# A graph network on one core: own messages transposed apart and joined on VectorE, one subtraction on GpSimd, shorter stage orders

## What is computed

```python
# layer 0 (twice): out[dst] = sum over edges of dinv[src]*dinv[dst]*(x @ W)[src], plus b
# layer 2:
att = sigmoid(xs @ W_att[:d] + xd @ W_att[d:] + b_att)     # xs = x[src], xd = x[dst]
messages = (xs @ W_msg + b_msg) * att
aggregated = segment_sum(messages, dst)
gi = aggregated @ W_ih.T + b_ih ;  gh = x @ W_hh.T + b_hh
r, z = sigmoid(i_r + h_r), sigmoid(i_z + h_z)
n = tanh(i_n + r * h_n)
h_new = (1 - z) * n + z * x                                # then batch norm over the nodes
# layer 3: segment_sum(x[src], dst) @ W_neigh.T + b_neigh + x @ W_self.T + b_self
```

## Time and profile before

| | |
|---|---|
| time, median of 3 runs | 5524.07 us (5515.52 to 5529.74) |
| the profiled execution: its own time, its span | 5528.89 us, 5527.1 us |
| mean granted TensorE clock in it | 0.956 |
| busy: PE, DVE, ACT, POOL | 87%, 70%, 49%, 55% |
| gcn_second, from 855 us | about 557 us |
| attend, from 3985 us | about 745 us |
| combine, from 4975 us to the end | 552 us |

### The profile page before, as it was taken

How to read it: one execution, slowest core, us unless ns; L and a number is a source line. 1 busy time by engine, 2 the same in 40 slices (tenths; PEclk the granted TensorE clock), 3 DMA queues, 4 the chain that set the end, 5 groups by cost and what they waited for, 6 DMA issues and landing times. The chain is left out here.

```text
span 5527.1 us, 107663 instructions
## 1 busy us (share of the span) xinstructions
PE 4833.4 (87%) x28685; PEld 3861.5 (70%) x28685; DVE 3842.1 (70%) x11930; ACT 2711.7 (49%) x6605; POOL 3016.8 (55%) x2962
## 2 busy tenths in 40 slices
PE   4499996666799989999999998888799999787887
PEld 4488885555688867777777775777566666676877
DVE  8567775776688855555555554788678888785766
ACT  2644444655433322222222222777677777573555
POOL 0177765777677743333433332777466665007776
PEclk9999997777899989999999998999999999998999
DMA  4889994554577754444444443788877666794554
GB/s 153 273 246 274 273 271 142 151 148 145 179 238 237 235 171 156 151 149 148 154 153 152 146 152 96 222 243 245 244 227 223 218 221 208 250 313 131 151 151 142
DMA packets 551179, 1075.25 MB, mean 195 GB/s; under 512 B 110995, under 2 KB 118202, under 8 KB 547962
## 3 DMA queue, kind: packets, MB, share of 16 engines
q1 hardware_dynamic: 451194, 854.46, 46.4%
q0 software_dynamic: 99840, 219.14, 16.1%
HBM read 712.24 MB, written 360.98 MB: 194 GB/s over the span
## 5 line engine op out<-in xcount | busy, mean ns | idle before, releaser
L841 POOL DMA_INDIRECT s_rows<-t_h,s_index x416 | 523.9, 1259 | 833.9 <-DVE s_index L834 732.9
L841 POOL DMA_INDIRECT g_rows<-t_x,g_index x416 | 426.8, 1026 | 382.3 <-issue 361.1
L841 POOL DMA_INDIRECT cb_rows<-t_x,cb_index x416 | 395.4, 950 | 432.0 <-DVE cb_index L834 309.8
L841 POOL DMA_INDIRECT at_rows<-t_m,at_index x416 | 434.5, 1044 | 301.1 <-DVE at_index L834 191.0
L841 POOL DMA_INDIRECT s_rows<-t_v,s_index x416 | 407.1, 979 | 211.5 <-issue 125.9
L841 POOL DMA_INDIRECT s_rows<-t_x,s_index x416 | 420.7, 1011 | 152.4 <-issue 118.2
L841 POOL DMA_INDIRECT g_rows<-t_h,g_index x416 | 402.3, 967 | 171.2 <-issue 124.4
L905 PE MATMUL bank<-s_onehot,s_hi 128*128 128x80 f32 (+9 forms) x1758 | 437.5, 289 | 48.8 <-DVE s_lo L876 27.3
L1724 DVE TENSOR_TENSOR s_rout<-bank,s_x 128x512 f32<-128x512 f32 x98 | 67.8, 692 | 586.9 <-PE bank L1668 586.9
L905 PE MATMUL bank<-g_onehot,g_rows 128*128 128x80 f32 (+9 forms) x1172 | 298.5, 420 | 195.0 <-DMA g_rows<-t_h,g_index 184.5
L905 PE MATMUL bank<-s_onehot,s_lo 128*128 128x80 f32 (+9 forms) x1758 | 432.0, 286 | 0.0
(11 more groups left out here) (335 smaller groups left out, 13286.1 us busy)
## 6 DMA issues: line engine op xcount, KB each, us to landing
s_scale<-inv_d SPq DMA_DIRECT2D x196, 256.0 KB
t_h<-s_hout SPq DMA_DIRECT2D x98, 512.0 KB
s_own<-t_h SPq DMA_DIRECT2D x98, 512.0 KB
t_m<-s_mout SPq DMA_DIRECT2D x98, 264.0 KB
at_own<-t_m SPq DMA_DIRECT2D x98, 264.0 KB
t_x<-so_x SPq DMA_DIRECT2D x98, 256.0 KB, 4.5
g_own<-t_x SPq DMA_DIRECT2D x98, 256.0 KB
g_scale<-dinv_d SPq DMA_DIRECT2D x98, 256.0 KB
```

The lines of the kernel that those rows point to most:

```text
L841: pool.indirect_dma_start(out=self.rows[:, self.ring(q) + k, :], out_offset=None, in_=self.table[0:NPAD, :], in_offset=bass.IndirectOffset ...
```

## The change

In `attend`: `mine` is no longer multiplied into the bank of the sums. A new TensorE piece `flip` transposes it into a bank of its own (bank 6), ACT `hold` now copies that bank to `own_t`, and a new VectorE piece `join` computes agg = own_t x own + sums in one pass out of the bank. The candidate's matmul of all tiles now goes to bank 5 (it was bank 5 or 6 in turn), so it waits for the blend of the tile just before. The subtraction x2 - n moves from VectorE's `move` to GpSimd's `part`, into a tile `diff`. r, z and n get four buffers each, and lags and list orders change. In `gcn_second` and `combine` only lags and orders change.

```diff
 # gcn_second
-                    (9, lambda q: store(sp, q, group_of(t_x1[0:NPAD, :], q.t), xout[q.u][:, :], ln.applied,
+                    (6, lambda q: store(sp, q, group_of(t_x1[0:NPAD, :], q.t), xout[q.u][:, :], ln.applied,
...
-                over_groups(pe, [(3, turn), (1, sums)])
+                over_groups(pe, [(1, sums), (2, turn)])
...
-                over_groups(act, [(2, hold), (4, weight), (6, lambda q: ln.root(act, q)), (8, apply)])
+                over_groups(act, [(2, hold), (4, lambda q: ln.root(act, q)), (3, weight), (5, apply)])
...
-                e.on_vector(dve, [(7, lambda q: ln.invert(dve, q)), (5, add), (0, lambda q: e.prepare(dve, q))])
+                e.on_vector(dve, [(0, lambda q: e.prepare(dve, q)), (4, lambda q: ln.invert(dve, q)), (3, add)])
 # attend
-                e.fetch(pool)
+                def part(q):
+                    pool.wait_ge(tanhed, q.t + 1)
+                    if not is_first(q.t):
+                        wait_for(pool, moved, q.t - 1)
+                    pool.tensor_tensor(diff[q.u][:, :], x2[q.d % XS][:, :], ng[q.r][:, :], ALU.subtract)\
+                        .then_inc(parted, 1)
+
+                over_groups(pool, [(0, lambda q: e.gather(pool, q)), (7, part)], XS)
...
-                                 (10, lambda q: store(sp, q, slab_of(hnt, q.t), hn[q.u][:, :], moved, stored))],
+                                 (11, lambda q: store(sp, q, slab_of(hnt, q.t), hn[q.u][:, :], moved, stored))],
...
                 def sums(q):
                     e.fetched(pe, q)
+                    if not is_first(q.t):
+                        pe.wait_ge(agged, q.t - 1)
+                    e.sum_by_feature(pe, q, [bank[q.u]]).then_inc(e.summed, 1)
+
+                def flip(q):
                     pe.wait_ge(mailed, q.t + 1)
-                    if not is_first(q.t):
-                        pe.wait_ge(agged, q.t - 1)
-                    e.sum_by_feature(pe, q, [bank[q.u]], close=False)
+                    if not (isinstance(q.t, int) and q.t < 1):
+                        pe.wait_ge(copied, q.t)
                     for b in range(BLK):
-                        last = pe.matmul(nodes(bank[q.u])[:, b, :], mine[q.u][:, b, :],
-                                         id_own[:, :], start=False, stop=(b == BLK - 1),
-                                         skip_group_check=True)
-                    last.then_inc(e.summed, 1)
+                        last = pe.transpose(bank[6][:, b * P:(b + 1) * P], mine[q.u][:, b, :], ident[:, :])
+                    last.then_inc(turned, 1)
...
-                    if not is_first(q.t):
-                        pe.wait_ge(mixed, q.t - 1)
-                    pe.matmul(bank[5 + q.u][:, :], wih_s[:, 2 * P:3 * P], agg[q.u][:, :], start=True, stop=True)\
+                    if not (isinstance(q.t, int) and q.t < 1):
+                        pe.wait_ge(mixed, q.t)
+                    pe.matmul(bank[5][:, :], wih_s[:, 2 * P:3 * P], agg[q.u][:, :], start=True, stop=True)\
                       .then_inc(joined, 1)
 
-                over_groups(pe, [(5, gates), (3, sums)], XS)
+                over_groups(pe, [(5, gates), (3, sums), (2, flip)], XS)
...
                 def hold(q):
-                    act.wait_ge(e.summed, q.t + 1)
-                    if not is_first(q.t):
-                        act.wait_ge(joined, q.t - 1)
-                    act.activation(planes(agg[q.u]), nodes(bank[q.u]), ACT.Copy).then_inc(agged, 1)
+                    act.wait_ge(turned, q.t + 1)
+                    if not is_first(q.t):
+                        act.wait_ge(agged, q.t - 1)
+                    act.activation(own_t[q.u][:, :], bank[6][:, :], ACT.Copy).then_inc(copied, 1)
...
-                over_groups(act, [(4, hold), (6, candidate), (1, open_), (2, weigh), (5, gate)], XS)
+                over_groups(act, [(3, hold), (6, candidate), (1, open_), (1, weigh), (5, gate)], XS)
...
+                def join(q):
+                    dve.wait_ge(copied, q.t + 1)
+                    dve.wait_ge(e.summed, q.t + 1)
+                    if not is_first(q.t):
+                        dve.wait_ge(joined, q.t - 1)
+                    dve.scalar_tensor_tensor(out=planes(agg[q.u]), in0=planes(own_t[q.u]), scalar=own[:, 0:1],
+                                             in1=nodes(bank[q.u]), op0=ALU.mult, op1=ALU.add).then_inc(agged, 1)
...
                 def move(q):
 
-                    dve.wait_ge(tanhed, q.t + 1)
+                    dve.wait_ge(parted, q.t + 1)
                     if not is_first(q.t):
                         dve.wait_ge(stored[q.u], q.n * 16)
-                    dve.tensor_tensor(hn[q.u][:, :], x2[q.d % XS][:, :], ng[q.u][:, :], ALU.subtract)\
+                    dve.tensor_tensor(hn[q.u][:, :], diff[q.u][:, :], zg[q.r][:, :], ALU.mult)\
                        .then_inc(link3, 1)
...
-                e.on_vector(dve, [(2, choose), (1, look), (6, move), (5, blend)], ahead=2)
+                e.on_vector(dve, [(4, join), (2, choose), (0, look), (7, move), (5, blend)], ahead=2)
 # combine
-                    (8, leave)])
+                    (6, leave)])
...
-                over_groups(pe, [(1, sums), (3, dense)])
+                over_groups(pe, [(1, sums), (2, dense)])
...
-                over_groups(act, [(2, hold), (5, lambda q: ln.root(act, q)), (7, apply)])
+                over_groups(act, [(2, hold), (4, lambda q: ln.root(act, q)), (5, apply)])
...
-                e.on_vector(dve, [(6, lambda q: ln.invert(dve, q)), (4, add), (0, lambda q: e.prepare(dve, q))])
+                e.on_vector(dve, [(0, lambda q: e.prepare(dve, q)), (4, lambda q: ln.invert(dve, q)), (3, add)])
```

More of the change, by code:

```diff
@@ L1897, in attend @@
             agg = ph.pair("agg", [P, GRP])
-            r, zg, mix, ng = (ph.pair(n, [P, GRP]) for n in ("r", "z", "mix", "n"))
+            own_t, diff, mix = (ph.pair(n, [P, GRP]) for n in ("own_t", "diff", "mix"))
+            r, zg, ng = (ph.pair(n, [P, GRP], n=4) for n in ("r", "z", "n"))
+            turned, copied, parted = ph.sem("turned"), ph.sem("copied"), ph.sem("parted")
             hn = ph.pair("hn", [P, GRP])
@@ L1990, in weigh @@
                     if not is_first(q.t):
-                        act.wait_ge(e.summed, q.t - 1)
+                        act.wait_ge(turned, q.t - 1)
                     for b in range(BLK):
@@ L1997, in hold @@
                 def hold(q):
-                    act.wait_ge(e.summed, q.t + 1)
+                    act.wait_ge(turned, q.t + 1)
                     if not is_first(q.t):
-                        act.wait_ge(joined, q.t - 1)
-                    act.activation(planes(agg[q.u]), nodes(bank[q.u]), ACT.Copy).then_inc(agged, 1)
+                        act.wait_ge(agged, q.t - 1)
+                    act.activation(own_t[q.u][:, :], bank[6][:, :], ACT.Copy).then_inc(copied, 1)
                 def gate(q):
                     act.wait_ge(crossed, q.t + 1)
-                    if not is_first(q.t):
-                        act.wait_ge(moved, q.t - 1)
+                    if not is_first(q.t, 4):
+                        act.wait_ge(moved, q.t - 3)
                     a, b = GATES[q.u]
-                    act.activation(r[q.u][:, :], bank[a][:, :], ACT.Sigmoid, bias=brz_c[:, 0:1])
-                    act.activation(zg[q.u][:, :], bank[b][:, :], ACT.Sigmoid, bias=brz_c[:, 1:2])\
+                    act.activation(r[q.r][:, :], bank[a][:, :], ACT.Sigmoid, bias=brz_c[:, 0:1])
+                    act.activation(zg[q.r][:, :], bank[b][:, :], ACT.Sigmoid, bias=brz_c[:, 1:2])\
                        .then_inc(opened, 1)
@@ L2013, in candidate @@
                     act.wait_ge(mixed, q.t + 1)
-                    act.activation(ng[q.u][:, :], mix[q.u][:, :], ACT.Tanh, bias=bih_c[:, 2:3])\
+                    act.activation(ng[q.r][:, :], mix[q.u][:, :], ACT.Tanh, bias=bih_c[:, 2:3])\
                        .then_inc(tanhed, 1)
-                over_groups(act, [(4, hold), (6, candidate), (1, open_), (2, weigh), (5, gate)], XS)
+                over_groups(act, [(3, hold), (6, candidate), (1, open_), (1, weigh), (5, gate)], XS)
             @block.vector
@@ L2042, in blend @@
                     dve.scalar_tensor_tensor(out=mix[q.u][:, :], in0=hx[q.d % XS][:, :], scalar=bhh_c[:, 2:3],
-                                             in1=r[q.u][:, :], op0=ALU.add, op1=ALU.mult).then_inc(link, 1)
+                                             in1=r[q.r][:, :], op0=ALU.add, op1=ALU.mult).then_inc(link, 1)
                     dve.wait_ge(link, q.t + 1)
                     dve.wait_ge(joined, q.t + 1)
-                    dve.tensor_tensor(mix[q.u][:, :], mix[q.u][:, :], bank[5 + q.u][:, :], ALU.add)\
+                    dve.tensor_tensor(mix[q.u][:, :], mix[q.u][:, :], bank[5][:, :], ALU.add)\
                        .then_inc(mixed, 1)
                 def move(q):
-                    dve.wait_ge(tanhed, q.t + 1)
+                    dve.wait_ge(parted, q.t + 1)
```

(9 more changed lines are left out.)

2 lines of the change are left out of this document (1 added, 1 removed).

## The result

| | before | after |
|---|---|---|
| median of the runs made side by side, us | 5525.59 (7 runs, 5515.52 to 5529.74) | 5542.50 (7 runs, 5537.01 to 5546.27) |
| the profiled execution, us | 5528.89 | 5546.27 |
| its span, us | 5527.1 | 5544.5 |

The ratio is 1.0029, with a 95% interval of 1.0018 to 1.0041: the kernel has become 17 us **slower**, at the edge of the 0.3% that the prediction named. The forecast was 5499 us, and faster.

What follows compares the result with a forecast made beforehand. Gathers were taken to bound gcn_second and combine, TensorE attend, and GpSimd attend after the change. The profiled 5528.9 us less 20 (attend) and 8 (ends) gave 5501, stated as 5499 us; range 5468 to 5544.

Steps and rivals of the forecast that it cites:

- Bound and waits before: Kernel before: gathers bound gcn_second and combine; TensorE bounds attend, busy all 600 us, at 7.23 us a tile.
- The four numbers close behind TensorE: Attend, us a tile: VectorE 6.35, ScalarE 5.59, GpSimd 5.8, the round over ScalarE and VectorE 6.7.
- 1, TensorE: Attend: four passes fewer save 0.45 us a tile, 44 us over 98 tiles; TensorE's tile becomes 6.78 us.
- 2, VectorE: Attend: subtraction of 0.691 us goes, join of 0.747 comes; VectorE's tile becomes 6.41 us.
- rival C: Attend: GpSimd's subtraction takes 1.16 us of VectorE every tile, giving 7.57 us a tile; slower, 5554 us; chance 0.13.
- 2, the waits on VectorE: Attend: the 42.9 us wait for the store goes; the join's wait for its tile's sums costs nothing.
- 3, ScalarE and bank 5: Attend: ScalarE's copy from bank 6 and bank 5 alone for the candidate cost nothing if the round stays under 6.78 us.
- 4, GpSimd: Attend: subtraction costs 1.46 us a tile between gathers, between 0.85 and 2.01; GpSimd sets the pace, attend ends 20 us earlier.
- 5, the ends: Ends of gcn_second and combine: fewer applies after the last root, 4 us each, 8 us together, between 0 and 12.

Runs made afterwards that it cites:

- e1: The changed kernel with only the subtraction back on VectorE, GpSimd only gathering; 5524.75 us, 0.9999 of the kernel before.
- e2: The kernel before with only the new lags and orders of gcn_second and combine, attend untouched; 5513.09 us, 0.9979 of the kernel before.
- f3: The changed kernel with the subtraction on VectorE and the own rows' load ahead of x2's; 5497.67 us, 0.9960 of the kernel before.
- f2: The changed kernel with only the subtraction back on VectorE, run in a later series; 5518.43 us, 0.9988 of the kernel before.
- f1: The changed kernel itself, run again as control in the later series; 5541.56 us, 1.0030 of the kernel before.
- f4: The changed kernel, GpSimd's subtraction included, with the own rows' load ahead of x2's; 5532.88 us, 1.0014 of the kernel before.
- e6: The kernel before with only the subtraction on GpSimd, r, z, n in four buffers, move and store a step later; 5526.02 us, 1.0000 of before.
- e5: The kernel before with new orders in gcn_second and combine, own messages as transposes adding into the bank of the sums; 5502.35 us, 0.9957.

## Why the prediction was wrong

By its own steps:

- **Bound and waits before**: right as far as they go. The four numbers close behind TensorE were what decided.
- **1, TensorE.** The four passes do span 0.47 us, and TensorE left its bound. None of the 44 us came through.
- **2, VectorE: the step that failed.** It set 6.35 + 0.06 = 6.41 us a tile and left the compares at their old length. Measured: join for subtraction is right (740 against 691 ns), but 1.16 us of compares come on top, for the 0.69 us that the subtraction saves. That is rival C in its mechanism: it took the length of GpSimd's pass as VectorE's loss and forecast 7.57 us a tile, where 7.55 was measured. It had a chance of 0.13. That its figures fit so closely is partly luck. Its 1.16 us was a guess at a pass that takes 1.30, of which nine tenths are lost. And the work under it was too high by a quarter of a us: what is measured is (600 - 18.1)/79.5 = 7.32 us a tile, 6.16 without the loss, in place of 6.41 (e1 says the same, 6.88 with the subtraction and 6.19 without), and the wait for the own rows, 0.23 us a tile, fills the gap. The argument against it, that gathers and VectorE get on well, was about another kind of work: the compares stay at 494 ns beside the gathers, and lengthen only beside a pass that reads operands from SBUF.
- **2, the waits on VectorE.** That the wait for the store would go was right (42.9 us, now none). But the change's later move also holds x2's buffer longer, the load of the own rows queues behind x2's on SyncE, and look wants them a step earlier: 18.1 us in 600, which no term had. The prediction asked only what stood behind the join.
- **3, ScalarE and bank 5**: put at nothing, and VectorE, which sets the tile, waits neither at the join (1.0 us) nor at the blend's second pass, which reads bank 5 (2.7 us). TensorE's and its loads' waits at that bank (L1979) are for VectorE's blend.
- **4, GpSimd.** The pass was taken as 1.16 + 0.30 = 1.46 us on top of the gathers and their gaps. It is 1.28 us and then 0.16 until the next gather, but it starts right behind the gather ahead of it, where the sum had already counted a gap of 0.30:

```profile
4301.82 0.94 POOL L841 DMA_INDIRECT at_rows<-t_m,at_index  x1 [0.30 <-issue]
4302.78 1.28 POOL L1919 TENSOR_TENSOR at_diff<-at_x,at_n 128x512 f32<-128x512 f32 x1
4304.23 1.05 POOL L841 DMA_INDIRECT at_rows<-t_m,at_index  x1 [0.16 <-issue]
```

  So a pass adds 0.02 + 1.28 + 0.16 - 0.30 = 1.16 us, under the 1.2 at which the prediction's own sum hands the bound from GpSimd back to TensorE. That GpSimd's queue would set the pace, the ground of the forecast, was wrong too. Its 692 us from first to last gather became 717, since it waited for n: it was not the bound.
- **5, the ends**: 8 us forecast, 12.6 measured by e2's medians, 9 in e2's own stages and 15 in the changed kernel's (gcn_second 9.4 and combine 5.7, against 4 each). The size was somewhat too small; how much, single profiles don't tell.

Together: attend +30 in place of -20, the ends -15 in place of -8, 3 elsewhere: +17. Rival C's 5554 us stands 8 us above the profiled 5546 (the ends 7 too small, attend 3 too large, and 3 elsewhere that it didn't have), and the median lies another 4 us lower. In parts of attend: with the subtraction on VectorE and the own rows first the stage is 13 us shorter than before (f3); the late own rows give 24 of that back (f2); GpSimd's pass takes another 21 (f1). Taken in the other order the pass costs 31 (f4) and the late own rows 14. The median of 5542.5 lies inside the range of 5468 to 5544, by 1.5 us; that is no merit of the mechanism, since the range reached up to most of rival C.

## What to carry to other kernels

Before moving a pass from VectorE to GpSimd, price it on VectorE as well. By these runs VectorE loses three quarters to nine tenths of a GpSimd pass that reads SBUF, wherever its own passes with two inputs in SBUF stand beside it: the move pays only if the pass saved on VectorE is longer than that, and it is free (e6) while VectorE has the time to spare and another engine is the bound. When a consumer moves a step later, its input's buffer comes free a step later too; look at what else stands behind that load on the queue, and at whether the same edit makes it wanted sooner. And two losses in a row hide each other: after the first is taken away, read the waits again.

## What was not expected of the hardware

- A write-only pass of GpSimd (1024 columns, 0.97 us) takes nothing from VectorE's compares, a copy of 0.65 us takes 0.50 us a tile, a subtraction of 1.30 us takes 1.16.
- The loss isn't a slowdown of several instructions: one compare beside the pass is held for about its whole length (0.55 us becomes 1.92), and its neighbours keep their lengths.
- In this contention GpSimd loses little: its subtraction takes at least 1270 ns in the changed kernel, 1282 in the median and 1622 at most.
- Behind its arithmetic pass GpSimd issues the next gather after 0.16 us, and the pass itself starts 0.02 us behind a gather; between two gathers lie 0.30.
- fp32 transposes in four weight loads (0.47 to 0.50 us) can add into a bank that already holds sums (e5); the products with a scaled identity take eight (0.97 us).
